# A fused token mixer, scan and expert kernel: attention's first pass of a later batch moved into the scan steps of an earlier one

## The chip, the cores and the metric

The kernel runs as one program on one core of one Trainium2 chip. The metric is device time in microseconds: the median of 3 runs is 1213.12 us (1211.83 to 1215.1). TensorE (PE in the profile), VectorE (DVE), ScalarE (ACT), GpSimd (POOL) and SyncE (SP) each run their own list of instructions in order and wait for one another by semaphores.

## The reference, cut to what matters

Four batches of 512 image tokens of width 256 go through attention with 16 heads of 16; 77 text tokens are then appended (589 rows, computed as 590), and a state-space layer with 16 states runs over them. Two expert layers and a causal attention follow; the change does not touch them except for the zeroing of their buffers in DRAM.

```
h = attention(x)                       # softmax(q k / 4) v, 16 heads, then w_out
h = concat([h, txt])
u = layernorm(h)
xp = u @ x_proj_w.T                    # 64 for the step size, 16 for B, 16 for C
delta = softplus(xp[:64] @ dt_proj_w.T + dt_proj_b)
for each t:  s = exp(delta*A)*s + delta*B_t*u_t ;  y_t = sum_n s*C_t
h = h + y + u * D_skip
h = h + one_expert(layernorm(h)) ; h = h + causal(layernorm(h)) ; h = h + two_experts(layernorm(h))
```

## The kernel before

Everything is written out by hand: each engine's list is a sequence of calls, and the semaphore waits stand in the functions. No scheduler moves anything.

**Attention of a batch** has two passes over 16 units (`NU`; 4 groups of 4 heads, `hg`, by 4 blocks of 128 tokens, `i`). In the first pass `scores` (PE, L646) writes two halves of a unit, each into a pair of PSUM banks, and `maxima` (DVE, L1588) takes the row maxima of a half. After each group `turn_maxima` (PE, L655) turns the maxima and `minus` (DVE, L1593) subtracts them inside Q. `project` (PE, L623) with `take_q` (ACT, L1163) makes Q and K of a group, `project_v` with `take_v` makes V. In the second pass `tscores` (PE, L741) makes the scores again, turned, `exps` (ACT, L1217) exponentiates them, and `weighted` (PE, L754) multiplies by V. `turn_heads`, `values`, `turn_values`, `take_vals`, `project_out` (PE, L789) and `residual` finish the batch. Then come the layer norm (`moments`, `standard_deviations`, `scales`, `normalise`), `turn_tokens`, `take_u`, `project_x`, `take_x`, `project_dt`, `softplus`, `step_size`, `input_size`.

**The scan of a batch** has 16 steps, one per state. In each, ACT makes `dA` (`decay`, L1208, L1209) and DVE runs `drive` (L1630), `recurrence` (L1639) and `output_gate` (L1649). For the first three batches POOL adds the result by DMA onto `yS` (even steps) or `yodd` (odd steps), and the gate two steps later waits for that DMA (`y_even`, `y_odd`); the last batch adds on PE. SP spreads B and C of each step over the partitions (`bc`, 4 slots).

**The order of the stages** is: first pass of batch 0 (`front(0, None)`), its second pass (`back(0, None)`), then for b = 0, 1, 2 `front(b + 1, b)`, the first pass of batch b+1 with what prepares scan b, and `back_ahead(b + 1, b)`, the second pass of batch b+1 under the 16 steps of scan b; at last scan 3 (`back(None, 3)`). The skip term u * D_skip is multiplied by PE (`skip`, L688) into the tail banks 5 to 7, and ACT copies it to `yS` (`take_y`) before POOL adds to it. `turn_both` (PE, L810, L811) turns `yS` and `yodd` back into the tail banks, and `add_y` (DVE, L1674, L1676) adds them to the hidden rows.

**The zero fills**: four DMAs (L478 to L484, the buffers of the two expert layers) are issued on SP after the load of batch 1's x.

Of the kernel before, what the change touches and what calls it, by code (L numbers as in the profile page):

```python
# [6 lines left out]
def fusion_kernel(nc, A, out):  # L7
# [41 lines left out]
    with ctx:  # L49
# [60 lines left out]
        uT = eb("uT", [P, KC, LP])  # L110
# [3 lines left out]
        eb("room", [P, 632])  # L114
# [5 lines left out]
        dBu = eb("dBu", [P, 3, KC, LP])  # L120
# [296 lines left out]
        QG = HG - 1  # L417

        def gap_bank(hg, which):
            return 5 + (2 * hg + which) % 3  # L420

        SETS = (0, 2, 5)

        def score_sets(b):
            return 3 if b == 0 else 2

        def score_banks(b, v):
            first = SETS[v % score_sets(b)]
            return slice(first, first + 2)

        def turned_banks(v):
            return slice(SETS[v % 3], SETS[v % 3] + 2)

# [12 lines left out]
        def _(q):  # L446
# [18 lines left out]
            def load_x(b):  # L465
                q.wait_ge(pe_v, 2 * b)
                q.dma_start(xT[:, :, :], A["xT"][b]).then_inc(x_in, 16)

            def spread(b, n):
                k = NS * b + n  # L470
                if k >= SLOTS:
# [6 lines left out]
            q.dma_start(xs_dram.rearrange("(j p) d -> p j d", p=P),  # L478
                        zeros[:, :].rearrange("p (o d) -> p o d", o=1).to_broadcast([P, MT, DW])).then_inc(zero_out, 16)
            q.dma_start(ys_dram.rearrange("(j p) d -> p j d", p=P),  # L480
                        zeros[:, 0:D].rearrange("p (o d) -> p o d", o=1).to_broadcast([P, G, D])).then_inc(zero_out, 16)
            q.dma_start(xs5_dram.rearrange("(j p) d -> p j d", p=P),
                        zeros[:, :].rearrange("p (o d) -> p o d", o=1).to_broadcast([P, NP2, DW])).then_inc(zero_out, 16)
            q.dma_start(ys5_dram.rearrange("(j p) d -> p j d", p=P),  # L484
                        zeros[:, 0:D].rearrange("p (o d) -> p o d", o=1).to_broadcast([P, 2 * G, D])).then_inc(zero_out, 16)
            for b in range(NB):
# [3 lines left out]
                if 0 < b < NB - 1:  # L490
                    q.wait_ge(dve_hC, NS * b)
# [110 lines left out]
        def _(pe):  # L602

            def project(b, hg, which, bank):
                if hg == 0 and which == 0:
                    pe.wait_ge(x_in, 16 * (b + 1))
                    if b == 0:
                        pe.wait_ge(wq_in, 16)
                    elif b == 1:
                        pe.wait_ge(dve_h1, 2 * b)  # L610
                    else:
                        pe.wait_ge(act_ys, b - 1)
                if b == 0 and hg == 1 and which == 0:
                    pe.wait_ge(wq_rest_in, 16)
                if b >= 2 and hg < QG and 2 * hg + which >= 3:
                    pe.wait_ge(act_q, 2 * HG * b + 2 * hg + which - 2)
                if bank == 4:
                    if which:
                        pe.wait_ge(act_q, 2 * (HG * b + hg) + 1)
                    elif hg > 1:  # L620
                        pe.wait_ge(dve_q, HG * b + hg - 1)
# [4 lines left out]
            def project_v(b, half):  # L626
                if half == 0:
                    pe.wait_ge(dve_q, HG * b + HG - 1)
                else:
                    pe.wait_ge(act_v, 2 * b + 1)  # L630
                for i in range(2):
                    for c in range(KC):
                        m = nc.tensor.matmul(ps[:, 4, D * i:D * (i + 1)], xT[:, c, P * (2 * half + i):P * (2 * half + i + 1)], wv[:, c, :],  # L633
# [1649 lines left out]
```

## Time and profile before

| | us |
|---|---|
| median of 3 runs | 1213.12 |
| span of the profiled execution | 1222.6 |
| PE, DVE, ACT busy in it | 929.1, 763.9, 440.4 |
| from the start to the end of scan 3's steps and y | 695 |
| the rest (experts, causal attention) | 527.6 |

For the profiled execution no time is given apart from its span; it is 9.5 us (0.8%) above the median of the runs. The stages before 695 us follow one another by DVE's instructions: first pass of batch 0 to 62.4, its second pass to 115, first pass of batch 1 to 181.8, scan 0 to 273.3, first pass of batch 2 to 336.2, scan 1 to 427.6, first pass of batch 3 to 490.5, scan 2 to 592.4, scan 3 to 695. A row of the view by stretches gives for each stretch the busy time of each engine, TensorE's granted clock as a share of 2.4 GHz, and the share of the DMA engines' time.

### The profile page before, as it was taken

The numbers are of one execution on the slowest core, as the hardware profiler recorded it, in microseconds if no ns is written. First come the engines' busy times: TensorE is split into PE (matmuls) and PEld (weight loads), VectorE is DVE, ScalarE is ACT, GpSimd is POOL, SyncE is SP. The second block draws the span as 40 slices with busy tenths as digits, with TensorE's granted clock in tenths as the row PEclk, the third lists the DMA queues.
The fourth block names the chain that finished last, engine by engine and source line by source line (L and its number), as shares of the span: only waits on it lengthen the run. The fifth ranks groups of instructions, "written<-read, shape, count | busy, mean of one in ns | idle before, by whom it ended". The sixth has DMA issues, their size and how long they took to land.

```text
span 1222.6 us, 14392 instructions
## 1 busy us (share of the span) xinstructions
PE 929.1 (76%) x4656; PEld 511.5 (42%) x4657; DVE 763.9 (62%) x1348; ACT 440.4 (36%) x819; POOL 205.3 (17%) x248
## 2 busy tenths in 40 slices
PE   6898989879888688974286529999588887548880
PEld 2323432334323243222253229998356565324440
DVE  4803589996899968999779931111467756732225
ACT  1174138750287501873352203444123331212220
POOL 1000001110011100111000142333000203355550
PEclk9989798976889858796687859999799998769995
DMA  3199206873058730597656436664501400249926
GB/s 100 27 326 330 84 23 160 212 166 100 18 151 206 172 109 1 135 213 159 160 181 211 148 128 192 196 195 149 233 1 46 179 6 14 75 140 398 402 75 253
DMA packets 75259, 185.57 MB, mean 152 GB/s; under 512 B 12010, under 2 KB 48573, under 8 KB 72512
## 3 DMA queue, kind: packets, MB, share of 16 engines
q1 hardware_dynamic: 60800, 148.11, 36.9%
q0 software_dynamic: 14400, 36.71, 13.7%
q8 instruction: 33, 0.54, 0.2%
q14 instruction: 26, 0.21, 0.1%
HBM read 124.88 MB, written 43.69 MB: 138 GB/s over the span
## 4 chain that ended last, share of the span: by engine, by line
PE 35%; DVE 29%; issue 19%; DMA 9%; POOL 3%; ACT 2%; another core or an unknown queue 1%; SPq 1%; POOLq 0%; DVEq 0%; ACTq 0%
DVE hst L1639 8%; PE ps L646 7%; DVE hC L1649 5%; PE ps L1139 5%; DMA bc<-bc_dram 4%; DVE mxn L1588 4%; PE ps L1015 3%; PE ps L623 3%; PE ps L1127 2%; POOL ys_dram L1546 2%; PE ps L1087 2%; DMA yodd<-hC 2%; PE ps L741 2%; DVE Hs L2170 1%; PE ps L633 1%
## 5 line engine op out<-in xcount | busy, mean ns | idle before, releaser
L1588 DVE TENSOR_REDUCE mxn<-ps 128x2 f32<-128x1024 f32 x128 | 150.6, 1220 | 60.3 <-PE ps L646 60.0
L1639 DVE TENSOR_TENSOR_SCAN hst<-dA,dBu 128x1180 f32<-128x1180 f32 x64 | 166.9, 2608 | 3.1 <-ACT dA L1209 2.6
L646 PE MATMUL ps<-Kh,Qh 32*128 32x512 f32 x512 | 122.6, 763 | 25.4 <-DVE mxn L1588 24.6
L1217 ACT ACTIVATE Ph<-ps 128x1024 f32<-128x1024 f32 x128 | 125.2, 1077 | 24.1 <-PE ps L741 23.5
L741 PE MATMUL ps<-Qh,Kh 32*128 32x512 f32 x512 | 111.0, 717 | 5.6 <-ACT Ph L1217 5.4
L1630 DVE TENSOR_TENSOR dBu<-dtu,bc 128x1180 f32<-128x1180 f32 x64 | 88.0, 1380 | 14.7 <-DMA bc<-bc_dram 14.5
L1649 DVE TENSOR_TENSOR hC<-hst,bc 128x1180 f32<-128x1180 f32 x64 | 87.2, 1362 | 9.6 <-DMA yodd<-hC 9.6
L1525 POOL DMA_DIRECT2D yS<-hC x24 | 20.8, 868 | 426.6 <-DVE hC L1649 426.6
L1139 PE MATMUL ps<-ring,xgT 128*64 128x256 f32 x512 | 70.1, 395 | 13.6 <-ACT xgT L1477 9.4
L1906 DVE TENSOR_TENSOR yo<-ps,b2r 128x256 f32<-128x256 f32 x32 | 13.6, 425 | 106.4 <-PE ps L938 106.4
L754 PE MATMUL ps<-Ph,Vh 128*32 128x512 f32 x512 | 73.7, 649 | 7.1 <-ACT OT L1221 4.4
L1208 ACT ACTIVATE dA<-delta,acol 128x590 f32<-128x590 f32 x64 | 52.2, 816 | 72.0 <-DVE hst L1639 66.1
L2163 DVE COPY yo<-ps 128x256 f32<-128x256 f32 x64 | 26.7, 423 | 77.2 <-PE ps L1139 62.3
L646 PEld LDWEIGHTS ps<-Kh,Qh 32*128 32x128 f32 x512 | 37.3, 213 | 87.2 <-DVE mxn L1588 65.7
L1577 POOL DMA_INDIRECT ys_dram<-yo,dest x64 | 62.4, 974 | 51.0 <-DVE yo L2163 31.2
L623 PE MATMUL ps<-xT,wqk 128*128 128x512 f32 x128 | 65.1, 649 | 7.6 <-DMA wqk<-in_wqk 5.6
L1557 POOL DMA_INDIRECT xs_dram<-xa,to x40 | 39.5, 988 | 175.1 <-DVE to L2005 161.9
L741 PEld LDWEIGHTS ps<-Qh,Kh 32*128 32x128 f32 x512 | 32.9, 202 | 80.8 <-ACT Ph L1217 42.0
L928 PEld LDWEIGHTS ps<-xgT,W 128*128 128x128 f32 x512 | 63.7, 196 | 3.4 <-ACT xgT L1354 1.8
L928 PE MATMUL ps<-xgT,W 128*128 128x128 f32 x512 | 64.3, 280 | 1.0 <-ACT xgT L1354 1.0
L763 PE MATMUL ps<-hC,ident 128*128 128x512 f32 (+1 forms) x96 | 45.8, 628 | 19.6 <-DVE hC L1649 19.6
L938 PE MATMUL ps<-W,hidT 128*128 x256 | 60.4, 379 | 0.0
(263 smaller groups left out, 1443.8 us busy)
## 6 DMA issues: line engine op xcount, KB each, us to landing
bc<-bc_dram SPq DMA_DIRECT2D x64, 590.0 KB, 5.9
ring<-in_we SPq DMA_DIRECT2D x16, 2048.0 KB
W<-in_w SPq DMA_DIRECT2D x46, 512.0 KB, 5.9
yS<-hC POOLq DMA_DIRECT2D x24, 590.0 KB, 7.9
yodd<-hC POOLq DMA_DIRECT2D x24, 590.0 KB, 7.8
xs_dram<-zeros SPq DMA_DIRECT2D x1, 8224.0 KB, 43.8
xg<-xs_dram SPq DMA_DIRECT2D x16, 514.0 KB
ys_dram<-zeros SPq DMA_DIRECT2D x1, 5120.0 KB, 48.3
```

The source lines that it names most:

```text
L623: m = nc.tensor.matmul(ps[:, bank, :], wqk[:, hg, which, c, :], xT[:, c, :], start=(c == 0), stop=(c == KC - 1))
L646: m = nc.tensor.matmul(ps[:, banks.start + hh % 2, :], Qh[HR * hh:HR * (hh + 1), hg, P * i:P * (i + 1)], Kh[HR * hh:HR * (hh + 1), hg, :], ...
L741: m = nc.tensor.matmul(ps[:, banks.start + hh % 2, :], Kh[HR * hh:HR * (hh + 1), hg, P * j:P * (j + 1)], Qh[HR * hh:HR * (hh + 1), hg, :], ...
L754: m = nc.tensor.matmul(ps[HR * hh:HR * (hh + 1), 4, :], Vh[:, j, 4 * hg + hh, :], Ph[:, n % 2, hh, :], start=(j == 0), stop=(j == QT - 1))
L928: m = nc.tensor.matmul(ps[:, 2 + u, P * f:P * (f + 1)], W1[:, v, c, P * f:P * (f + 1)], xgT[:, u, c, :], start=(c == 0), stop=(c == KC - 1))
L1139: t = nc.tensor.matmul(ps[CAP * k:CAP * (k + 1), 2 + j % 4, 0:D], xgT5[:, j % 2, c, CAP * k:CAP * (k + 1)], weights_of(g % PLACES)[:, 2 * ...
L1217: nc.scalar.activation(Ph[:, n % 2, 2 * g:2 * g + 2, :], ps[:, turned_banks(2 * n + g), :], ACT.Exp, scale=float(HD) ** -0.5).then_inc(act ...
L1577: nc.gpsimd.indirect_dma_start(ys5_dram, bass.IndirectOffsetOnAxis(dest5[:, j:j + 1], 0), yo5[:, j // GP % YG, j % GP, :], None, bounds_ch ...
L1588: nc.vector.tensor_reduce(slots32(mxn[:, hg % 2, i, :])[:, 2 * g:2 * g + 2, HD], ps[:, score_banks(b, 2 * (QT * hg + i) + g), :], AX.X, AL ...
L1630: nc.vector.tensor_tensor(dBu[:, k % 3, :, :], dtu[:, :, :], bc[:, k % SLOTS, 0:1, :].to_broadcast([P, KC, LP]), ALU.mult).then_inc(dve_dB ...
L1639: nc.vector.tensor_tensor_scan(hst[:, k % 2, :, :].rearrange("p c t -> p (c t)"), dA[:, k % 2, :, :].rearrange("p c t -> p (c t)"), dBu[:, ...
L1649: nc.vector.tensor_tensor(hC[:, k % 2, :, :], hst[:, k % 2, :, :], bc[:, k % SLOTS, 1:2, :].to_broadcast([P, KC, LP]), ALU.mult).then_inc( ...
```

## The change

1. The first pass of a batch no longer has a stage of its own, except batch 0's (`first_maxima`). Units 0 to 4 of batch 1 run under the second pass of batch 0, units 5 to 11 between it and scan 0 (`first_attention`), and units 12 to 15 in steps 0 to 3 of scan 0. Steps 4 to 15 of scan b take units 0 to 11 of batch b+2, steps 0 to 3 of the next scan its units 12 to 15 (`unit_at`, `LAG`).
2. From batch 1 on, all halves use one pair of banks (6, 7), except odd halves of units 6 to 11 of batch 1; projections and turned maxima use bank 5. The second pass has two pairs (0, 1 and 2, 3) where it had three.
3. In a scan step DVE runs `maxima` before `recurrence` and again before `output_gate`; `drive` of the next step moves to the end of the step. `dBu` has 2 buffers for 3, `uT` 2 for 1.
4. Skip term: `skip` and `take_y` of batches 0 to 2 go. `turn_both` multiplies u by the diagonal of D as a third matmul, in three rounds (tokens 0 to 255, 256 to 511, the text rows), in steps 1 and 2 of the next scan; `add_y` has a part for each round. POOL's first two transfers of a scan are plain copies that wait for the last round.
5. The four zero fills are issued on ACT, behind the scale of A and ahead of `take_q(0, 1, 0)`, and no longer on SP. SP no longer waits for the end of a scan before the next one's first spreads.

ScalarE at the start of the program, before (Q and K are the outputs of `take_q`, group 0, then group 1 and on):

```order
L1163 ACTIVATE Qh<-ps,bqk 128x512 [waits pe_q,pool_init,bqk_in]
L1163 ACTIVATE Kh<-ps,bqk 128x512 [waits pe_q]
L1485 ACTIVATE acol<-alog 128x32 [waits consts_in]
L1163 ACTIVATE Qh<-ps,bqk 128x512 [waits pe_q]
L1163 ACTIVATE Kh<-ps,bqk 128x512 [waits pe_q]
```

ScalarE at the same place, after:

```order
L1233 ACTIVATE Qh<-ps,bqk 128x512 [waits pe_q,pool_init,bqk_in]
L1233 ACTIVATE Kh<-ps,bqk 128x512 [waits pe_q]
L1542 ACTIVATE acol<-alog 128x32 [waits consts_in]
L1543 DMA xs_dram<-zeros 128x32x257
L1545 DMA ys_dram<-zeros 128x20x256
L1547 DMA xs_dram<-zeros 128x64x257
L1549 DMA ys_dram<-zeros 128x40x256
L1233 ACTIVATE Qh<-ps,bqk 128x512 [waits pe_q]
```

The four transfers now stand between the two groups' Q and K.

VectorE in the first steps of scan 0, before (no maxima stand between scans):

```order
L1630 TENSOR_TENSOR dBu<-dtu,bc 128x1180 [waits dve_scan,bc_in2]
L1639 SCALAR_TENSOR_TENSOR hst<-dA,dBu 128x1180 [waits dve_hC,act_dA,dve_dBu]
L1649 TENSOR_TENSOR hC<-hst,bc 128x1180 [waits y_even,dve_scan]
L1630 TENSOR_TENSOR dBu<-dtu,bc 128x1180 [waits dve_scan,bc_in3]
L1639 SCALAR_TENSOR_TENSOR hst<-dA,dBu 128x1180 [waits dve_hC,act_dA,dve_dBu]
```

VectorE in steps 1 and 2 of scan 1, after (mxn are maxima, Hs the rows that a round of y is added to):

```order
L1646 TENSOR_REDUCE mxn<-ps 128x2 [waits pe_s]
L1697 SCALAR_TENSOR_TENSOR hst<-dA,dBu 128x1180 [waits dve_hC,act_dA,dve_dBu]
L1646 TENSOR_REDUCE mxn<-ps 128x2 [waits pe_s]
L1707 TENSOR_TENSOR hC<-hst,bc 128x1180 [waits y_even,dve_scan]
L1735 TENSOR_TENSOR Hs<-Hs,ps 128x512 [waits pe_yt]
L1688 TENSOR_TENSOR dBu<-dtu,bc 128x1180 [waits dve_scan,bc_in2]
L1646 TENSOR_REDUCE mxn<-ps 128x2 [waits pe_s]
L1697 SCALAR_TENSOR_TENSOR hst<-dA,dBu 128x1180 [waits dve_hC,act_dA,dve_dBu]
L1735 TENSOR_TENSOR Hs<-Hs,ps 128x512 [waits pe_yt]
L1646 TENSOR_REDUCE mxn<-ps 128x2 [waits pe_s]
```

Two maxima and, here, a round of y have joined each step; each waits for PE.

TensorE around the second round of y in step 1 of scan 1, after (L664 are scores, L748 turned scores, L762 the weighted sum, L826 to L828 the turning of y):

```order
L664 MATMUL ps<-Kh,Qh 128x512 [waits dve_max]
L664 MATMUL ps<-Kh,Qh 128x512
L748 MATMUL ps<-Qh,Kh 128x512 [waits act_p]
L748 MATMUL ps<-Qh,Kh 128x512
L762 MATMUL ps<-Ph,Vh 32x512 [waits act_p]
L762 MATMUL ps<-Ph,Vh 32x512 x3
L826 MATMUL ps<-ident,yS 128x128 [waits dve_h2]
L827 MATMUL ps<-ident,yodd 128x128
L828 MATMUL ps<-dskd,uT 128x128
```

The round waits on DVE's previous `add_y`, and the next step's scores are queued behind it; in the old order nothing of a scan step stood behind a turning.

The diff, cut to its core:

```diff
@@ banks
-        SETS = (0, 2, 5)
+        OWN, SPARE = (6, 7), (3, 4)
+        MISC = 5
+        LAG = 4
+        SOLO = 5
+        Y_ROUNDS = ((0, 2), (2, 4), (4, 5))
+        def score_pair(b, u, g):
+            if b == 0:
+                return FIRST_SETS[(2 * u + g) % 3]
+            return SPARE if b == 1 and g == 1 and SOLO < u < NU - LAG else OWN
+        def unit_at(eb, n):
+            return (eb, NU - LAG + n) if n < LAG else (eb + 1, n - LAG)
@@ sync
-            q.dma_start(xs_dram..., zeros...)
-            q.dma_start(ys_dram..., zeros...)
-            q.dma_start(xs5_dram..., zeros...)
-            q.dma_start(ys5_dram..., zeros...)
-                if 0 < b < NB - 1:
-                    q.wait_ge(dve_hC, NS * b)
@@ tensor
+            def turn_both(b, r):
+                if r == 0:
+                    pe.wait_ge(y_even, 8 * NS * (b + 1))
+                    pe.wait_ge(y_odd, 8 * NS * (b + 1))
+                if b < NB - 2:
+                    if r == 0:
+                        pe.wait_ge(dve_q, HG * (b + 2) + QT - 1)
+                    else:
+                        pe.wait_ge(dve_h2, y_count(b, r - 1))
+                elif r == 2:
+                    pe.wait_ge(dve_h2, y_count(b, 0))
...
+                        nc.tensor.matmul(dst, yS[:, c, tokens], ident[:, :], start=True, stop=False)
+                        nc.tensor.matmul(dst, yodd[:, c, tokens], ident[:, :], start=False, stop=False)
+                        m = nc.tensor.matmul(dst, uT[:, b % 2, c, tokens], dskd[:, c, :], start=False, stop=True)
+            def during_scan(cb):
+                eb, ab = cb + 1, cb + 2
+                for n in range(NS):
+                    b, v = unit_at(eb, n)
+                    units = list(units_ahead(n))
+                    for part in range(2):
+                        if b < NB:
+                            scores(b, v, part)
+                        for u in units[part:part + 1]:
+                            tscores(eb, u)
+                            if u:
+                                weighted(eb, u - 1)
+                        if part == 0:
+                            if n == 9:
+                                weighted(eb, NU - 1)
+                            if n % QT == 0 and (n < 8 or ab < NB):
+                                turn_maxima(eb if n < 8 else ab, (2, 3, 0, 1)[n // QT])
+                            if n == 11:
+                                project_out(eb, 0)
+                                project_out(eb, 1)
+                            if n == 13:
+                                turn_tokens(eb)
+                            if n == 14:
+                                project_dt(eb)
...
+                        if n % QT == 3 and ab < NB:
+                            project(ab, n // QT, part)
@@ scalar
+            act.dma_start(xs_dram..., zeros...)
+            act.dma_start(ys_dram..., zeros...)
+            act.dma_start(xs5_dram..., zeros...)
+            act.dma_start(ys5_dram..., zeros...)
+            first_maxima()
@@ scalar, at the end of a step of during_scan
+                    if n % QT == 3 and ab < NB:
+                        take_q(ab, n // QT, 0)
+                        take_q(ab, n // QT, 1)
@@ gpsimd, add_state
-                if n == 0:
-                    pool.wait_ge(act_ys, b + 1)
+                if n < 2 and b:
+                    pool.wait_ge(pe_yt, y_count(b - 1, 2))
@@ vector
+            def during_scan(cb):
+                for n in range(NS):
+                    b, v = unit_at(eb, n)
+                    if b < NB:
+                        maxima(b, v, 0)
+                    recurrence(cb, n)
+                    if n % QT == 0 and (n < 8 or ab < NB):
+                        minus(eb if n < 8 else ab, (2, 3, 0, 1)[n // QT])
...
+                    if b < NB:
+                        maxima(b, v, 1)
+                    if n:
+                        output_gate(cb, n - 1)
...
+                    if n + 1 < NS:
+                        drive(cb, n + 1)
+                    else:
+                        step_size(eb)
+                output_gate(cb, NS - 1)
+                input_size(eb)
+                drive(eb, 0)
```

## Rows read from the trace of the kernel before

**Rows 1.** The page, chain that ended last, shares by engine.

```profile
PE 35%; DVE 29%; issue 19%; DMA 9%; POOL 3%; ACT 2%; another core or an unknown queue 1%; SPq 1%; POOLq 0%; DVEq 0%; ACTq 0%
```

**Rows 2.** Busy by stretch: length, PE, PEld, DVE, ACT, POOL, PEclk, DMA share, GB/s.

```profile
62.40:115.00 52.60, 48.37 (x302) 16.80 (x295) 5.59 (x21) 34.37 (x39) 0.00 (x0) 0.92 1.09 320
115.00:181.80 66.80, 58.67 (x225) 24.62 (x228) 42.71 (x40) 19.76 (x30) 0.00 (x0) 0.88 0.26 90
181.80:273.30 91.50, 75.76 (x354) 27.28 (x346) 87.22 (x69) 65.16 (x87) 12.84 (x15) 0.85 0.74 176
273.30:336.20 62.90, 55.47 (x216) 25.66 (x218) 46.58 (x54) 7.26 (x12) 0.86 (x1) 0.74 0.22 63
336.20:427.60 91.40, 71.65 (x354) 26.03 (x346) 87.45 (x69) 65.82 (x87) 12.57 (x15) 0.89 0.74 176
490.50:592.40 101.90, 67.19 (x322) 24.70 (x314) 90.29 (x71) 63.39 (x84) 13.43 (x16) 0.73 0.76 181
```

**Rows 3.** What DVE waited for, whole span: us in total, times, longest.

```profile
DVE mxn L1588 <- PE ps L646: 60.0, 46, 6.9
DVE rsum L1658 <- PE ps L771: 42.9, 1, 42.9
```

**Rows 4.** SP's queue in order of time: start us, us, what.

```profile
57.55 0.43 SPq L478 DMA_DIRECT2D xs_dram<-zeros  x1
58.02 10.21 SPq L480 DMA_DIRECT2D ys_dram<-zeros  x1
68.27 8.86 SPq L482 DMA_DIRECT2D xs_dram<-zeros  x1
77.17 27.73 SPq L484 DMA_DIRECT2D ys_dram<-zeros  x1
```

**Rows 5.** The page's DMA issues: KB each, us from issue to landing.

```profile
ys_dram<-zeros SPq DMA_DIRECT2D x1, 5120.0 KB, 48.3
```

**Rows 6.** ACT in order of time, at the start of the program.

```profile
13.51 0.23 ACT L1485 ACTIVATE acol<-alog 128x32 f32<-128x32 f32 x1 [1.85 <-DMA alog<-in_alog]
20.13 0.69 ACT L1163 ACTIVATE Qh<-ps,bqk 128x512 f32<-128x512 f32 x1 [6.39 <-PE ps L623]
```

**Rows 7.** DVE in order of time: maxima, a `minus`, a scan step, scan 0's first recurrence.

```profile
24.18 4.62 DVE L1588 TENSOR_REDUCE mxn<-ps 128x2 f32<-128x1024 f32 x4 [0.63 <-PE ps L646]
28.72 0.68 DVE L1593 TENSOR_TENSOR Qh<-Qh,ps 128x512 f32<-128x512 f32 x1
...
184.35 2.61 DVE L1639 TENSOR_TENSOR_SCAN hst<-dA,dBu 128x1180 f32<-128x1180 f32 x1
...
193.26 2.61 DVE L1639 TENSOR_TENSOR_SCAN hst<-dA,dBu 128x1180 f32<-128x1180 f32 x1
195.78 1.36 DVE L1649 TENSOR_TENSOR hC<-hst,bc 128x1180 f32<-128x1180 f32 x1
197.06 1.38 DVE L1630 TENSOR_TENSOR dBu<-dtu,bc 128x1180 f32<-128x1180 f32 x1
```

**Rows 8.** PE in order of time, at either clock.

```profile
21.09 1.98 PE L623 MATMUL ps<-xT,wqk 128*128 128x512 f32 x4
78.77 1.14 PE L741 MATMUL ps<-Qh,Kh 32*128 32x512 f32 x8
79.84 1.06 PE L754 MATMUL ps<-Ph,Vh 128*32 128x512 f32 x8
192.83 2.09 PE L741 MATMUL ps<-Qh,Kh 32*128 32x512 f32 x8
194.85 1.94 PE L754 MATMUL ps<-Ph,Vh 128*32 128x512 f32 x8
238.00 5.25 PE L789 MATMUL ps<-wo,valsT 128*128 128x256 f32 x16
```

**Rows 9.** What DVE waited for in scan 2, its steps (493.1 to 577) and its end.

```profile
DVE dBu L1630 <- DMA bc<-bc_dram: 4.8, 5, 1.7
...
DVE hC L1649 <- DMA yodd<-hC: 6.5, 1, 6.5
```

More of the change, by code:

```diff
@@ L602, in _, with project @@
         def _(pe):
-            def project(b, hg, which, bank):
+            def project(b, hg, which):
+                bank = MISC if b else which if hg == 0 else 4
                 if hg == 0 and which == 0:
@@ new lines, in skip, with first_maxima @@
+                        nc.tensor.matmul(tail[:, lo:hi], dskd[:, c, :], uT[:, b % 2, c, lo - c * LP:hi - c * LP],
+                                         start=(lo % S == 0 or lo == S), stop=False, skip_group_check=True)
+            def first_maxima():
+                b = 0
+                project(b, 0, 0)
+                project(b, 0, 1)
+                pe.wait_ge(consts_in, 16 * N_CONSTS)
+                for c in range(KC):
+                    m = nc.tensor.matmul(ps[:, 7, 0:D], bvb[:, c, :], wo[:, c, :], start=(c == 0), stop=(c == KC - 1))
+                m.then_inc(pe_bo, 1)
+                for u in range(NU):
+                    hg, i = u // QT, u % QT
+                    scores(b, u, 0)
+                    scores(b, u, 1)
+                    if i == 0 and hg:
+                        turn_maxima(b, hg - 1)
+                    if i in (1, 2):
+                        if hg + 1 < HG:
+                            project(b, hg + 1, i - 1)
+                        else:
+                            project_v(b, i - 1)
+                turn_maxima(b, HG - 1)
@@ new lines, in last_scan @@
+            def last_scan():
+                b = NB - 1
+                skip(b)
+                for r in range(len(Y_ROUNDS)):
+                    turn_both(b - 1, r)
+                for n in range(NS):
+                    if 0 <= n - 1 < NPF:
+                        route_turn(n - 1)
+                    if 0 <= n - 2 < NPF:
+                        route_logits(n - 2)
+                    if n == 11:
+                        route_rank(0)
+                    if n >= 2:
+                        add_state(b, n - 2)
+                add_state(b, NS - 2)
+                add_state(b, NS - 1)
+                turn_y(b)
@@ L1160, in _, with take_q @@
         def _(act):
-            def take_q(b, hg, which, bank):
+            def take_q(b, hg, which):
+                bank = MISC if b else which if hg == 0 else 4
                 act.wait_ge(pe_q, 2 * (HG * b + hg) + which + 1)
@@ L1703, in back_ahead, with first_attention @@
-            def back_ahead(eb, cb):
-                drive(cb, 0)
-                for n in range(NS):
-                    if n + 1 < NS:
-                        drive(cb, n + 1)
+                    unit_maxima(0, u)
+                    if u % QT == 0 and u:
+                        minus(0, u // QT - 1)
+                minus(0, HG - 1)
+            def first_attention():
+                for u in range(SOLO):
+                    unit_maxima(1, u)
+                minus(1, 0)
+                maxima(1, 5, 0)
+                values(0)
+                maxima(1, 5, 1)
+                maxima(1, 6, 0)
+                residual(0)
+                moments(0)
+                maxima(1, 6, 1)
+                maxima(1, 7, 0)
+                scales(0)
+                maxima(1, 7, 1)
+                maxima(1, 8, 0)
+                minus(1, 1)
+                maxima(1, 8, 1)
+                unit_maxima(1, 9)
+                unit_maxima(1, 10)
+                step_size(0)
+                maxima(1, 11, 0)
+                input_size(0)
+                maxima(1, 11, 1)
+                drive(0, 0)
```

629 lines of the change are left out of this document (295 added, 334 removed).

## The prediction

> **What bounds the kernel now.** I read the chain of waits first: PE 35% and DVE 29% of it, ACT 2% [rows 1], so the end is set by PE and DVE handing work to each other. The view by stretches then shows two kinds of stage. In a scan DVE is busy 87.2 of 91.5 us [rows 2]: it is the bound. In a first pass between scans DVE is busy 46.6 of 62.9 us, in batch 1's 42.7 of 66.8 [rows 2]; the waits say for what: 60.0 us in 46 waits of the maxima on the scores [rows 3]. Under the second pass of batch 0 DVE is busy 5.6 of 52.6 us, with one wait of 42.9 us [rows 2, 3]. So DVE idles in the first passes and in the first attention, not in the scans, and the change puts the first passes into the scans. The SP queue has its own reading: the four zero fills keep it for 10.2, 8.9 and 27.7 us each after a first of 0.4 [rows 4]. On SP nobody waited.
>
> **Zero fills on ScalarE: +41.** The four are issued one after another, each starting where the one before ends [rows 4]: 57.55 to 104.90, 47.3 us. The last one landed 48.3 us after its start [rows 5], that is at 125.5, and the DMA share in that stretch is 1.09 [rows 2]. So the issuing queue is held while the DMA engines are full; it is not a matter of an instruction's own cost. Queues run in order, so whatever stands behind these on an engine waits. In the new order that is `take_q(0, 1, 0)`. ACT would be free for the DMAs at 13.8 (scale of A from 13.51, 0.23 long) and is needed again at 20.13 [rows 6]. Held from 13.8 for 47.3 us it is free at 61.1: 41.0 us late. What is queued behind: PE's `project(0, 1, 1)` waits for that Q, and behind it all scores from the second half of group 0 on, so DVE's maxima run dry. Nothing covers it: no other work of the first pass is ready. The bounds are 0 (ACT's queue takes the DMAs as the first was taken, 0.43 each, done by 15.6, before 20.13) and 41; the nearest rows, the same four transfers in the same order, stand at 41, and I take that. That SP loses them is worth nothing: its next transfer is B and C of batch 0, after `take_x`.
>
> The Trainium skill, page "DMA: Bandwidth & Descriptors", section "Issuing engines are not separate DMA queues", says that starting DMAs on several engines saves only the sequencer's time of starting them, which is usually small relative to the DMA itself. By that rule the hold would be near 0 and the sum 41 lower. The trace disagrees for these transfers: the last held its queue 27.7 of its 48.3 us.
>
> **From the end of the first pass to scan 0: -14.** Before, scan 0's first recurrence starts at 184.35 [rows 7]. After, PE is the bound of the first attention: it is busy 48.4 of 52.6 already [rows 2]. It gets 10 halves of scores (a half is half of the 1.14 of the same shape [rows 8]: 5.7 us), 4 projections of 1.92 (the 1.98 less an overlap: 7.7) and two waits of 2 for ACT's copy: 17 us longer. Two bank pairs for three cost little: while ACT exponentiates a half (34.4 us for 39 instructions [rows 2], 0.9 each) PE fills the other in 0.57. In the stretch behind it, 66.8 long with PE busy 58.7 [rows 2], PE loses those 13.4 us, units 12 to 15 (4.6), the skip (about 2.3, the columns of 1.2 projections) and two turns of maxima (1.3): 21.6; that is the least it gets shorter. The most is 36: 18 of 32 halves go, and DVE's 24 idle us there with them as far as they were waits for scores. Net the bounds are -5 and -19. The chain of layer norm, u, x and step size keeps its order in it, and the last group's Q, K and V still go one by one through PE and ACT (four times 1.9 + 0.7); I take -14, nearer the end that takes the waits away, since the remaining halves of units 6 to 11 still alternate two bank pairs.
>
> **Scans 0 and 1: -12.7 and -3.2.** A step of DVE alone is 5.10 us: recurrence 2.52 and gate 1.28 from start to start, drive 1.30 (its 1.38 less the same overlap) [rows 7]. Two maxima at 1.15 (4.62 for 4) make it 7.4. The floor of the new stage is the DVE work of the two old ones [rows 2]. Scan 1: 87.5 + 46.6 = 134.1 against 91.4 + 62.9 = 154.3 (batch 3's first pass taken as batch 2's). Scan 0 has no y of an earlier batch to add; that work is 46.6 less 32 maxima (36.8), 4 `minus` (0.6 each, 2.4) and two operations of a drive's shape (2.8): 4.6. So its floor is 129.2 against 154.4. What is late on top of that, in one scan:
> - Steps 4 and 8 open a head group whose Q and K are copied at the end of the step before, behind that step's Exps: maxima 1.15, scores 0.57, unit of the second pass 2.07 (1.07 + 1.00 [rows 8]), two Exps 1.8, copy 0.69 [rows 6], projection 1.92, copy 0.69, scores 0.57 = 9.5 for a step of 7.4: 2.1 twice, 4.2.
> - Step 11: the second half's scores stand behind the projection out (twice a projection's columns, so 3.8 at full clock; 5.25 in the row [rows 8]) and a projection: 1.4 to 5.3 late, taken 3.
> - Steps 13 and 14, the same behind u, x and step size: 2.
> - The last gate waits for the DMA of step 13, as it did 6.5 us in scan 2 [rows 9]; the maxima now stand between, so 1.5.
> - At a scan's start the clock can be at the lower level, as in the rows at 192.83 and 194.85 [rows 8], where a step of PE (scores 2.09, 1.78 units at 3.9) is 9.0, over 7.4: 1.8 for one step.
>
> Sum 12.5. In scan 1 the three rounds of y add 4.5: round 1 waits for DVE's add at the end of step 1, a full round follows (the 12 matmuls of 128 columns and their weights, some 2.6), and the next scores stand behind it; step 2 the same. Scan 0: 129.2 + 12.5 = 141.7, -12.7; scan 1: 134.1 + 17 = 151.1, -3.2. Bounds: with no lateness -25.2 and -20.2; with PE at the lower clock through steps 0 to 8, 9 x 1.6 = 14 more each. The skip matmuls and the ACT copies that go were beside maxima and cost nothing.
>
> **Scan 2: +14.9.** No batch 4 exists, so only 8 maxima (9.2), 2 `minus` (1.2) and the y of batch 1 (4.6) join 90.3: floor 105.3 against 101.9. Lateness: y 4.5, last gate 4 (of 0 to 6.5), spreads 3 (they were 4.8 [rows 9], and the steps are short again): 11.5. So 116.8, +14.9; bounds +3.4 and +20.
>
> **Scan 3: +1.7.** The first drive now belongs to the stage before (-1.3); the y of batch 2 is turned after its last DMA has landed, with DVE's two adds at step 1, a step earlier than before: +3 (0 to 6). The rest of the kernel, 527.6 us, is unchanged: 0.
>
> **Sum.** 41.0 - 14 - 12.7 - 3.2 + 14.9 + 1.7 = +27.7. The profiled span would go from 1222.6 to 1250.3; the runs' median lies 9.5 below that execution, and the same difference gives 1213.1 + 27.7 = 1240.8, so 1241.
>
> **Rivals.**
> - *The hold does not occur on ScalarE* (chance 0.15). For it: no row shows a DMA issued there, and the first transfer took 0.43 us. Against: rows 4, the same transfers. Then 1241 - 41 = 1200; with the lateness cut too, down to 1160. The page's rule above is this rival.
> - *The hold occurs, but the steps are DVE-bound with little lateness* (0.10). For it: PE at full clock needs 1.14 + 1.78 x 2.07 = 4.8 of 7.4 us a step. All floors give -19 - 25.2 - 20.2 + 3.4 - 1.3 = -62, with the hold -21: 1192, and half the lateness 1215.
> - *TensorE falls to the lower clock in the scans* (0.12), ending slower still: scores alone between 273.3 and 336.2 had a mean of 0.74 [rows 2], and the new steps thin PE out. From 7.4 us on PE's 9.0 decides: 14 + 14 and up to 9 before scan 0 (-14 to -5): 1241 + 37 = 1278; 1260 if half of it comes.
> - *The edit of stages gives nothing at all* (0.05): the hold alone, 1254.
>
> The forecast as worked out, 1218 to 1260, has 0.58. The range that should hold the time 8 in 10 is 1193 to 1260: it takes in the first two rivals' middles and leaves out the full lower clock and the deepest gains. Within 0.3% is 1209.5 to 1216.8, what a measurement can hardly tell from no change: 0.05. Faster: 0.13 of the first rival and 0.07 of the second, 0.20. Slower: 0.75.
>
> **What would show it.** In the new profile: the four DMA issues on ACT's queue, 47 us in sum, the fourth near 28; group 1's first Q copy at about 61 and not 20; one DVE wait of about 40 us on scores near 22. DVE's first recurrence at about 184 - 14 + 41 = 211; from there to the next scan's 142, then 151, then 117. Maxima waiting on scores at steps 4, 8, 11 of scans 0 and 1 and at steps 2 and 3 behind y. Wrong if ACT's issues are under 1 us each (then 1200), or if a scan stage takes over 160 with PE at 0.5.

## The result, and the profile after

The changed kernel took 1270.47 us (median of 4, 1265.57 to 1274.11) beside 1212.47 of the kernel before: 1.048, interval 1.0446 to 1.0521, slower. I had forecast 1241. Four more executions gave 1263.1 beside 1212.65, 1.044 (1.0405 to 1.0482). So the change costs 50 to 58 us, not 28; the direction was right, and the time lies outside my range of 1193 to 1260.

The chain of waits of the changed kernel, shares of the span; ACT's queue, which had no share [rows 1], now has 4%:

```profile
PE 40%; DVE 27%; issue 17%; DMA 4%; ACTq 4%; POOL 3%; ACT 3%; another core or an unknown queue 1%; SPq 1%; POOLq 0%; DVEq 0%
```

ACT and its queue at the start of the program (start us, us, what), to be read against [rows 4, 6]:

```profile
12.12 0.23 ACT L1542 ACTIVATE acol<-alog 128x32 f32<-128x32 f32 x1 [0.81 <-DMA alog<-in_alog]
12.12 0.44 ACTq L1543 DMA_DIRECT2D xs_dram<-zeros  x1
12.60 9.28 ACTq L1545 DMA_DIRECT2D ys_dram<-zeros  x1
21.91 8.49 ACTq L1547 DMA_DIRECT2D xs_dram<-zeros  x1
30.43 28.20 ACTq L1549 DMA_DIRECT2D ys_dram<-zeros  x1
58.67 0.69 ACT L1233 ACTIVATE Qh<-ps,bqk 128x512 f32<-128x512 f32 x1 [46.33 <-issue]
```

The four issues follow one another to 58.6, and the first Q copy of group 1 stands behind them: 58.67 and not 20.13. "46.33 <-issue" is how such a hold shows: the engine sat idle and no releaser is named, and what fills the idle time are rows of its own queue. DVE ran dry behind it (DVE in order of time):

```profile
64.45 4.62 DVE L1646 TENSOR_REDUCE mxn<-ps 128x2 f32<-128x1024 f32 x4 [42.29 <-PE ps L664]
```

The stretches (columns as in [rows 2]): batch 0's first pass while held, its remainder, the first attention, the stretch to scan 0's first recurrence, scans 0, 1, 2, and 3 to its last recurrence.

```profile
13.80:62.40 48.60, 8.48 (x32) 2.78 (x24) 7.01 (x7) 0.69 (x1) 0.00 (x0) 0.59 1.09 299
62.40:102.60 40.20, 34.52 (x157) 14.04 (x160) 32.46 (x30) 4.63 (x7) 0.00 (x0) 0.97 0.46 157
102.60:161.90 59.30, 53.22 (x317) 15.96 (x309) 13.04 (x13) 34.68 (x39) 0.00 (x0) 0.98 0.00 1
161.90:215.00 53.10, 45.88 (x178) 22.30 (x174) 27.84 (x40) 17.00 (x27) 0.00 (x0) 0.84 0.16 55
215.00:361.00 146.00, 119.25 (x517) 45.79 (x514) 128.96 (x108) 75.34 (x99) 13.29 (x16) 0.83 0.52 126
361.00:521.40 160.40, 130.76 (x574) 55.74 (x574) 133.19 (x124) 72.86 (x97) 13.09 (x16) 0.81 0.50 125
521.40:644.40 123.00, 79.92 (x414) 36.66 (x414) 105.68 (x98) 64.87 (x87) 13.10 (x16) 0.79 0.64 163
644.40:732.00 87.60, 57.50 (x231) 37.13 (x231) 81.21 (x68) 30.82 (x51) 0.98 (x1) 0.81 0.59 198
```

The DVE work of scans 0 and 1, 129.0 and 133.2, is what I had summed as floors (129.2, 134.1); what is long is the rest. DVE's waits in scans 0, 1 and 2, one row each (us, times, longest):

```profile
DVE mxn L1646 <- PE ps L664: 20.0, 9, 5.3
DVE mxn L1646 <- PE ps L664: 26.9, 10, 5.3
DVE mxn L1646 <- PE ps L664: 13.1, 4, 5.3
```

(3.1 of the first stand just ahead of scan 0's first recurrence.) Two such waits. First, step 11 of scan 0 on PE in order of time: the second half's scores, at 315.15, stand behind a projection out at the lower clock and a projection, and DVE's maxima start at 316.32 after 5.29 us.

```profile
305.02 2.08 PE L664 MATMUL ps<-Kh,Qh 32*128 32x512 f32 x4
307.02 6.48 PE L795 MATMUL ps<-wo,valsT 128*128 128x256 f32 x16
313.34 1.88 PE L637 MATMUL ps<-xT,wqk 128*128 128x512 f32 x4
315.15 1.13 PE L664 MATMUL ps<-Kh,Qh 32*128 32x512 f32 x4
```

Second, step 1 of scan 1: round 0 of y holds PE from 370.92 to 375.2 ahead of scores, and rounds 1 and 2 each wait for DVE's add of the round before, while the next scores stand behind them.

```profile
376.46 1.23 DVE L1646 TENSOR_REDUCE mxn<-ps 128x2 f32<-128x1024 f32 x1 [5.25 <-PE ps L664]
...
383.68 1.23 DVE L1646 TENSOR_REDUCE mxn<-ps 128x2 f32<-128x1024 f32 x1 [2.81 <-PE ps L664]
...
392.14 1.23 DVE L1646 TENSOR_REDUCE mxn<-ps 128x2 f32<-128x1024 f32 x1 [4.14 <-PE ps L664]
```

```profile
370.92 0.80 PE L826 MATMUL ps<-ident,yS 128*128 128x128 f32 x2
...
379.63 0.49 PE L826 MATMUL ps<-ident,yS 128*128 128x128 f32 x2 [1.36 <-DVE Hs L1735]
...
388.06 0.71 PE L826 MATMUL ps<-ident,yS 128*78 128x128 f32 x2 [2.58 <-DVE Hs L1735]
```

### The profile page after: what moved, and what is told of

The parts are those of the page before. It is cut to its first block, busy times and chain, and to the rows that moved or that the text cites. A ratio compares the mean times of both kernels' runs of the same rounds, so it can differ in the third digit from the quotient of the medians.

```text
span 1265.5 us, 14467 instructions
## 1 busy us (share of the span) xinstructions
PE 927.3 (73%) x4692; PEld 517.8 (41%) x4693; DVE 763.7 (60%) x1351; ACT 440.6 (35%) x816; POOL 204.0 (16%) x248
## 4 chain that ended last, share of the span: by engine, by line
PE 40%; DVE 27%; issue 17%; DMA 4%; ACTq 4%; POOL 3%; ACT 3%; another core or an unknown queue 1%; SPq 1%; POOLq 0%; DVEq 0%
DVE hst L1697 7%; PE ps L664 6%; PE ps L1209 5%; DVE mxn L1646 4%; PE ps L637 4%; DVE hC L1707 3%; PE ps L748 3%; PE ps L1085 3%; PE ps L762 3%; ACTq L1549 2%; PE ps L1197 2%; PE ps L1157 2%; POOL ys_dram L1604 2%; DVE dBu L1688 2%; DMA yodd<-hC 1%
## 5 line engine op out<-in xcount | busy, mean ns | idle before, releaser
L1646 DVE TENSOR_REDUCE mxn<-ps 128x2 f32<-128x1024 f32 x128 | 154.1, 1219 | 173.0 <-PE ps L664 172.9
L664 PE MATMUL ps<-Kh,Qh 32*128 32x512 f32 x512 | 149.0, 723 | 53.9 <-DVE mxn L1646 46.0
L748 PE MATMUL ps<-Qh,Kh 32*128 32x512 f32 x512 | 132.7, 700 | 4.9 <-ACT Ph L1289 4.7
L637 PE MATMUL ps<-xT,wqk 128*128 128x512 f32 x128 | 71.1, 685 | 53.0 <-ACT Qh L1233 46.8
L664 PEld LDWEIGHTS ps<-Kh,Qh 32*128 32x128 f32 x512 | 40.0, 206 | 130.7 <-DVE mxn L1646 88.2
L762 PE MATMUL ps<-Ph,Vh 128*32 128x512 f32 x512 | 75.1, 662 | 1.3 <-ACT Ph L1289 1.3
L1635 POOL DMA_INDIRECT ys_dram<-yo,dest x64 | 62.2, 972 | 47.1 <-DVE yo L2266 26.7
L748 PEld LDWEIGHTS ps<-Qh,Kh 32*128 32x128 f32 x512 | 44.5, 207 | 46.7 <-issue 23.3
L637 PEld LDWEIGHTS ps<-xT,wqk 128*128 128x128 f32 x128 | 24.7, 212 | 94.4 <-ACT Qh L1233 57.6
```

The costliest lines, as they stand in the source:

```text
L637: m = nc.tensor.matmul(ps[:, bank, :], wqk[:, hg, which, c, :], xT[:, c, :], start=(c == 0), stop=(c == KC - 1))
L664: m = nc.tensor.matmul(ps[:, banks.start + hh % 2, :], Qh[HR * hh:HR * (hh + 1), hg, P * i:P * (i + 1)], Kh[HR * hh:HR * (hh + 1), hg, :], ...
L748: m = nc.tensor.matmul(ps[:, banks.start + hh % 2, :], Kh[HR * hh:HR * (hh + 1), hg, P * j:P * (j + 1)], Qh[HR * hh:HR * (hh + 1), hg, :], ...
L762: m = nc.tensor.matmul(ps[HR * hh:HR * (hh + 1), 4, :], Vh[:, j, 4 * hg + hh, :], Ph[:, n % 2, hh, :], start=(j == 0), stop=(j == QT - 1))
L1635: nc.gpsimd.indirect_dma_start(ys5_dram, bass.IndirectOffsetOnAxis(dest5[:, j:j + 1], 0), yo5[:, j // GP % YG, j % GP, :], None, bounds_ch ...
L1646: nc.vector.tensor_reduce(slots32(mxn[:, hg % 2, i, :])[:, 2 * g:2 * g + 2, HD], ps[:, score_banks(b, u, g), :], AX.X, ALU.max, negate=Tru ...
```

## The experiments

**e1, e2: the fills alone.** e1 is the changed kernel with them on SP, e2 the kernel before with them on ScalarE.

```diff
-            act.dma_start(xs_dram..., zeros...)      # e1: these four go
+            q.dma_start(xs_dram..., zeros...)        # e1: behind load_x(1), on SP; e2 the reverse
```

> The changed kernel with its four zero fills issued from SP's queue again, behind the load of batch 1, all else as changed. Theory A (the issues hold ScalarE's queue, and all behind it is late by that): the first pass of batch 0 ends 40.2 us earlier, at 62.4, nothing behind it gives that back, and the time is 1270.5 - 40.2 = 1230. Theory B (the fills cost by their traffic, wherever they are issued): the first pass keeps most of the 40 us and the time stays near 1270. Either way what is over 1212.5 is the price of the rest of the change: 18 us by A.

> The kernel before with one part of the change alone: the four zero fills issued by ScalarE behind the scale of A, ahead of the Q copies. Theory A: ScalarE held from 12.1 to 58.6 as in the changed kernel, 40 us on the end of the first pass, 1212.5 + 40 = 1252.5. Theory B: the hold costs only together with the new stages (the old ones would take it in their idle time): under 10 us, near 1215.

e1: 1222.8, 1.009 of before (1.0054 to 1.0124). Its first pass ends at 61.9, as before, and all stages behind are those of the changed kernel within 3.1 us. e2: 1247.9, 1.030 (1.0234 to 1.0356), its first pass ends 36.4 later. ScalarE's queue in e2:

```profile
12.47 8.84 ACTq L1480 DMA_DIRECT2D ys_dram<-zeros  x1
21.34 8.05 ACTq L1482 DMA_DIRECT2D xs_dram<-zeros  x1
29.42 25.31 ACTq L1484 DMA_DIRECT2D ys_dram<-zeros  x1
54.77 0.69 ACT L1155 ACTIVATE Qh<-ps,bqk 128x512 f32<-128x512 f32 x1 [42.56 <-issue]
```

Theory A stands both ways. Over the kernel before, the hold costs 37 us in the old order (e2, +36.9) and 39 to 46 in the new (+50.5 or +58.0, less e1's +11.8); the end of the first pass moves by 36 and 40. The traffic by itself cost nothing that is seen. The rest of the change costs 12 us, where I had forecast a gain of 13.

**e5: the changed kernel again.** No edit.

> The changed kernel, unchanged, beside the others of this call, to have its time and the kernel's before over more executions on one chip. If the 15 us between the difference of the two profiled executions (+42.9) and of the medians (+58.0) is scatter between executions, more of them give between the two, near 1211 + 50; if it is steady, +58 again.

1263.1, +50.5: the first reading. Scan 1 took 154.9 here, at a granted clock of 0.85, and 160.4 at 0.81 in the first profile, of the same kernel.

**e6: two fills on ScalarE, two on SP.**

```diff
-            act.dma_start(xs5_dram...)  act.dma_start(ys5_dram...)
+            q.dma_start(xs5_dram...)    q.dma_start(ys5_dram...)
```

> The changed kernel with the first two zero fills on ScalarE as in it and the last two on SP. Theory A (each issue is held until the transfer before it has been worked off, so the second takes 9.3, the third and fourth 8.5 and 28.2): ScalarE free at 22 where it is needed at 20.1, 1.8 late, some 1224. Theory B (the hold depends on all the bytes under way, from whichever queue): SP's two make the second issue on ScalarE longer, up to the 37 us of the four: 1224 to 1260.

1230.9, 1.016 (1.0126 to 1.0187). ScalarE and its queue:

```profile
13.15 0.44 ACTq L1547 DMA_DIRECT2D xs_dram<-zeros  x1
13.63 8.80 ACTq L1549 DMA_DIRECT2D ys_dram<-zeros  x1
22.48 0.69 ACT L1237 ACTIVATE Qh<-ps,bqk 128x512 f32<-128x512 f32 x1 [9.10 <-issue]
```

The second issue is held nearly as long as with all four on the queue (8.80 for 9.28), and the first pass ends at 65.2, 3.3 late. Theory B was not put to the test: SP issued its two from 61.33 us on, 39 us after ScalarE was free, so none of SP's fills was under way beside them. They show the same once more: the first of them (8.2 MB) took SP's queue 0.43, the second 25.4. The first issue on a queue is nearly free, the next ones are held. The time is 7 over theory A's 1224; the first pass, 3.3 late for 1.8, explains 1.5 of that, the rest stays open.

**e3: one bank pair in the kernel before**, for the scores of batches 2 and 3.

```diff
-            return 3 if b == 0 else 2
+            return 3 if b == 0 else 2 if b == 1 else 1
```

> The kernel before with the scores of batches 2 and 3 on one pair of banks instead of two in turn, so that the two halves of a unit are issued apart, each behind the maxima of the other. Theory A (a half that is issued by itself takes TensorE 1.1 us, as long as both halves issued together): a half costs 1.15 of maxima, 1.13 of scores and some 0.1 between them, 32 halves 76 us against a first pass of 62.9: 13 longer in each of two, 1238. Theory B (a half is half of the 1.14, 0.57): 32 x 1.8 = 58, under the 62.9 that the stage takes for other reasons: 0 to +3, 1212 to 1216.

1326.1, 1.092: stages 0 and 1 took 212.4 and 211.7 for 154, 58 longer each. Both theories missed the size; A's direction holds. PE in order of time:

```profile
305.87 2.08 PE L646 MATMUL ps<-Kh,Qh 32*128 32x512 f32 x4 [1.33 <-DVE mxn L1588]
...
309.27 2.08 PE L646 MATMUL ps<-Kh,Qh 32*128 32x512 f32 x4 [1.33 <-DVE mxn L1588]
```

A half by itself (x4) takes 2.08, what both halves (x8) of the same shape take at that clock in [rows 8]; a half goes round in 3.40, not the 2.4 I expected: the granted clock was 0.50 from 300 to 320 us, and PE stood idle 1.33 of each 3.40 of these rows. I had priced the alternation at the higher clock; at the lower 32 x 3.40 = 109 for 62.9, and more where y and projections stand between.

**e4: the y rounds' matmuls** cut to 3 a round on top of e1 (the kernel leaves out most of y of batches 0 and 1).

```diff
-                for i in range(first, last):
+                for i in range(first, last if b == NB - 2 else first + 1):
```

> As the first of these (fills on SP), and the matmuls that add and turn y of batches 0 and 1 cut from 12, 12 and 6 to 3 in each round (so most of that y is left out); the waits of the rounds, the adds of DVE and the order stay. Theory A (the three rounds' matmuls on TensorE, at either clock, stand ahead of scores for 12 us a scan in scans 1 and 2): some 10 less in each, 20 under the first kernel, 1210. Theory B (they cost the 4.5 that I put in the sum): 4 less in each, 1222. Theory C (it is the wait of a round for DVE's add, not the matmuls): hardly any change, 1228.

1214.6, 8 under e1; scan 2 went from 123.2 to 116.8, scan 1 from 160.4 to 154.9. Since e5 has 154.9 in scan 1 with all matmuls in, only scan 2's 6.4 (four executions of three kernels with the full rounds gave 123.0 to 123.2) is shown. That is between A and B. The maxima of scan 2 waited 8.4 in place of 13.1, and the last gate's wait of 2 for a DMA was gone; the 8.4 stay with the order.

**e7, e8: the late steps and the rounds' order.** e7 moves projections away from steps 7 and 11 and the Q copy ahead of the second unit's Exps; e8 also moves rounds 1 and 2 by half a step.

```diff
-                        if n % QT == 3 and ab < NB:
+                        if n in (3, 6, 10, 15) and ab < NB:          # V: both halves in step 9
...
-                            for r in ((0, 1), (2, None))[n - 1][part:part + 1]:
+                            for r in ((0, None), (1, 2))[n - 1][part:part + 1]:   # e8
```

> Fills on SP, and in the scans the first pass's projections placed away from the late steps: Q and K of the second head group at step 6 for 7, V in one step (9), Q and K of the third at step 10 for 11, where the projection out stands, and the Q copies at steps 3 and 6 between the two units' Exps. Theory A (steps 4, 8 and 11 are late, 2.8, 2.7 and 5.3 us, by what stands ahead of their scores on TensorE and ScalarE): about 6 to 7 of these 10.8 go in each of scans 0 and 1, 13 in all, 1222.8 - 13 = 1210. Theory B (TensorE is the bound over these steps, so the wait turns up at another): 0 to -3, 1220 to 1223.

> As e7, and the second and third rounds of y half a step later: the second ahead of the second unit part of step 2, the third behind it, so that neither waits for DVE's add of the round before while scores stand behind it. Theory A (the wait of a round for the add is a part of the y rounds' 10 to 12 us): 2 to 3 less in each of scans 1 and 2, 5 under e7. Theory B (TensorE's work alone decides, at the lower clock at a scan's start): no difference from e7.

e7: 1212.2, 0.999 (0.9969 to 1.002), 10.6 under e1; scan 0 fell from 146.0 to 141.1, scan 1 to 150.3. In scan 0 the wait of step 4 went from 2.8 to 1.8, those of steps 8 and 11 (2.7 and 5.3) are gone, and two of about 1 at step 6 came. Mostly A. e8: 1197.3, 0.990 (0.9843 to 0.9956). Its scan 2 took 114.2 for 120.2: the same matmuls, and 6 us less. What DVE's maxima waited for in e7 and then e8, 460 to 580 us (scan 2 starts at 468.5 and 460.6; 1.3 of the first row stand at the end of scan 1):

```profile
DVE mxn L1652 <- PE ps L672: 11.9, 5, 4.3
```

```profile
DVE mxn L1652 <- PE ps L672: 5.2, 2, 4.3
```

So in scan 2 the handing over between PE's rounds and DVE's adds cost as much as the matmuls; A, and larger than I had expected of it. In scan 1 no gain is shown. The waits of steps 1 and 2 went there too (2.8 and 2.7), but in two of three executions of this kernel (e8, e9, e14) that of step 6 grew from 0.7 to 3.4, and scan 1 took 148.7, 150.3 and 150.3 for e7's 150.3; since e7's had a granted clock of 0.85 and theirs 0.82, whether the order gives nothing there or the clock took it back stays open. Nor are the 15 us between the medians of e7 and e8 the edit's: scan 0, which it does not touch, took 136.1 in e8's profile and 141.1 in those of e7, e9 and e14.

**e9 to e12.** e9 is e8 again; e10 and e11 keep PE busy with dropped matmuls in its waits; e12 moves round 0 too.

```diff
+                        if part and n in (0,):          # e11: (0, 12)
+                            keep_busy(4 if n == 0 else 6)
...
-                            for r in ((0, None), (1, 2))[n - 1][part:part + 1]:
+                            for r in ((None, 0), (1, 2))[n - 1][part:part + 1]:   # e12
```

> e8 unchanged, over five rounds, since its one profiled execution was also shorter in stages that its edit does not touch (scan 0 by 5.0, the stretch ahead of it by 3.9 against e7). Theory A: the edit gives 6 in scan 2 and some 4 in scan 1, 10 under e7, 1202. Theory B (e8's 1197 is what it is): 1197. Both below the kernel before at 1211 to 1213.

> e8 with four matmuls of 128 x 512 into an unused bank, their result dropped, in TensorE's wait of 4.1 us ahead of the second score half of step 0 of scans 0, 1 and 2. Theory A (TensorE goes on at the lower clock because it stood idle there, and the scores, the turned scores and the first y round of step 1 then take 2.08, 3.8 and 4.2 us for 1.13, 2.0 and 2.6): the granted clock of the ten us behind rises from 0.5, and 3 to 5 us go in each of the three scans, 1197 - 12 = 1185. Theory B (the clock there has been lowered by what was before and does not come back by this): no gain, 1197, or a loss of 1 each where the four run at the lower clock and outlast the wait: 1200.

> As e10, with six more such matmuls in the wait of 5.6 us ahead of the second score half of step 12 in scans 0 and 1. Theory A: turning the tokens, the x projection (4.34 us in the row, for some 2.3) and the step size projection run at the higher clock, the waits of step 13 (1.0 to 1.5) go, 1 to 2 under e10 in each of two scans: 1182. Theory B: no difference from e10, or 1 to 2 more.

> As e8, with the first round of y half a step later too, behind the second score half of step 1. Theory A (the 4.3 to 5.2 us wait of step 1 is the round standing ahead of scores): that wait falls to about 1, of which the scores of step 2, now right behind the round, give back some 2: 2 less in each of scans 1 and 2, 1193. Theory B (TensorE is the bound from step 0 to step 3 whatever the order): 1197.

These ran on a chip where the kernel before took 1192.2, so only ratios are compared (the stages up to scan 3 took what they do elsewhere; the difference is in the rest, 513 in e9 and 536 in e14): e9 0.988 (0.9846 to 0.9913), e10 0.991, e11 0.991, e12 0.989, the last three within e9's interval. e8 stays under the kernel before. PE in e10, at the start of scan 1:

```profile
304.70 3.60 PE L885 MATMUL ps<-wqk 128*128 128x512 f32 x8
308.96 1.13 PE L672 MATMUL ps<-Kh,Qh 32*128 32x512 f32 x4 [0.66 <-DVE mxn L1658]
313.19 1.22 PE L672 MATMUL ps<-Kh,Qh 32*128 32x512 f32 x2 [3.11 <-DVE mxn L1658]
```

With the filler in the wait the next half ran at the higher clock, 1.13 (in e8, behind a wait of 4.09, it took 2.07), but behind the next wait, 3.11, the units ran at the lower clock as in e8: theory B in the time. In e12 step 1's wait on scores fell from 4.3 to 1.5, and DVE waited 2.2 for the round in its add: the wait changed its place, B again.

**e13, e14: three pairs.** What was still open was the stretch ahead of scan 0. e14 is e8 beside it.

```diff
+                scores(1, 6, 1)
                 project_out(0, 0)
                 project_out(0, 1)
-                scores(1, 6, 1)
...
+                scores(1, 8, 1)
                 turn_maxima(1, 1)
-                scores(1, 8, 1)        # and (11, 1) ahead of project(1, 3, 1)
```

> As e8, with the two halves of batch 1's units 6, 8 and 11, which have a bank pair each, issued back to back in the stretch behind the first attention, and the projections out, the turned maxima and the K projection that stood between them behind both. Nothing is added or removed. Theory A (a half issued alone takes TensorE as long as both together, 1.13 at the higher clock and 2.08 at the lower, not half of it, and that is what the prediction missed in this stretch): three such halves go, 1.13 + 2.08 + 1.13 = 4.3 of TensorE, of which 2 to 4 on the path, since it is busy 48.7 of 57.0 there; the stretch from the end of the first pass to the first recurrence falls from 112 or 116 to about 110 or 113. Theory B (a half costs the same wherever it stands): no change, or 1 to 2 longer where DVE now waits for the projection out.

> e8 unchanged, on the same chip as e13, since e13's edit is worth a few us and the same kernel took 112 in one profiled execution and 116 in another over the stretch in question: about 0.988 of the kernel before, as it was.

e13 0.988 (0.9839 to 0.9918), e14 0.9935 (0.9902 to 0.9967): the intervals overlap, and the medians are 1199.5 and 1200.85, so the times alone show no difference. (e14, forecast at 0.988, came out nearer to 1.) From the first pass's end to the first recurrence the two took 111.4 and 114.7, closer than e8 and e9, which are one kernel (112.2 and 116.1). The traces are clearer where they are cut at the end of the first attention. From there to the first recurrence (columns as in [rows 2]), e14 and then e13:

```profile
122.10:174.92 52.82, 45.62 (x174) 22.34 (x174) 27.70 (x39) 16.97 (x27) 0.00 (x0) 0.84 0.15 55
```

```profile
124.80:173.13 48.33, 40.69 (x176) 21.18 (x174) 27.61 (x39) 16.97 (x27) 0.00 (x0) 0.89 0.16 59
```

This part took 52.8 to 53.3 in each of the twelve profiled executions of the changed order without e13's edit, and 48.3 with it: 4.5 less, with TensorE busy 4.9 less. The scatter stands in the first attention itself, 58.3 to 63.6. PE in e14 and in e13, unit 8:

```profile
145.95 2.08 PE L672 MATMUL ps<-Kh,Qh 32*128 32x512 f32 x4
147.96 1.11 PE L690 MATMUL ps<-ident,mxn 128*128 128x128 f32 x4
149.00 2.08 PE L672 MATMUL ps<-Kh,Qh 32*128 32x512 f32 x4
```

```profile
148.69 2.09 PE L672 MATMUL ps<-Kh,Qh 32*128 32x512 f32 x8
150.72 1.11 PE L690 MATMUL ps<-ident,mxn 128*128 128x128 f32 x4
```

Two halves apart: 4.16. Back to back: 2.09. Theory A, in the trace. Three halves are 4.3 of the 4.9; the rest goes with the higher granted clock, 0.89 for 0.84. e8 and all that is built on it stay under the kernel before, by 0.7 to 1.2%.

## Why the prediction was wrong, step by step

The direction was right by the hold alone: without it I had forecast a gain of 13 and measured a loss of 12 (e1). Single profiled executions of one kernel differ by up to 6 us in one stage, so I take means: of the old order over the kernel before, e2 and e3 (in stages that their edits leave alone), of the new over the first profile, e1, e5 and e6. Stages run between first recurrences.

| stage | old, us | new, us | difference | predicted |
|---|---|---|---|---|
| first pass to its last `minus` | 61.9 | 101.9 | +40.0 | +41 |
| to scan 0 | 119.9 | 115.1 | -4.8 | -14 |
| scan 0 | 154.1 | 145.6 | -8.5 | -12.7 |
| scan 1 | 155.2 | 158.1 | +2.9 | -3.2 |
| scan 2 | 99.7 | 123.1 | +23.4 | +14.9 |
| scan 3, to its last recurrence | 89.7 | 87.7 | -2.0 | +1.7 |
| rest | 533.4 | 534.0 | +0.6 | 0 |
| sum | | | +51.6 | +27.7 |

Of the 23.9 missed, 14.6 stand in scans 1 and 2, 9.2 in the stretch to scan 0 and 4.2 in scan 0; the hold, scan 3 and the rest give 4.1 back.

- **The hold (+41) was right**, in mechanism and size (+40.0), against the rival without it: e1 and e2. Here the Trainium skill, page "DMA: Bandwidth & Descriptors", section "Issuing engines are not separate DMA queues", has the starting of a DMA cost a usually small sequencer time; the rows bear that out for the first issue (0.44) and not for those behind it (9.3, 8.5, 28.2).
- **In the stretch to scan 0 the step that failed is "a half is half of the 1.14"**, and with it the choice of -14. A half issued alone takes 1.13 or 2.08, as long as the pair. The Trainium skill, page "TensorEngine Tiling (Array Packing)", section "Key Properties", says that tiles of the array can run matmuls in parallel; the rows agree (x8 in 1.14, x4 in 1.13), and read ahead of the prediction it would have spoken against halving. So would the trace of the kernel before: from 115 to 181.8 its scores took TensorE 26.7 us for 32 halves, 0.83 each.

  To compare my two parts, the stage has to be cut at the same work, the last weighted sum of batch 0: the 52.6 of [rows 2] also hold the turning of the heads and the projection out, which now stand behind the first attention. Cut there, in means over the same executions, the first attention grew from 40.0 to 61.4, by 21.5 where I had 17, and the stretch behind it fell from 79.3 to 53.0, by 26.3 where I had 31. In the first part a half straight ahead of turned scores runs partly within them: a unit with one takes 2.9 to 3.2 for 2.07, so 0.8 to 1.1 for a half and not 0.57, by this estimate some 4 over the ten, about what was missed. In the second part, in the first profile, 8 halves between 161.9 and 215 stand alone, five at 1.13 and three at 2.08: 11.9 where eight at 0.57 are 4.6. e13 shows that this lies on the path, by undoing three for 4.5 us.

  That is not a full account of the second part. The halves that left it had cost more than 0.57 too, so the scores fell by 10.0 (26.7 to 16.7) for the 10.3 of the sum: there two errors met, which is luck. All of TensorE's work fell by 24.4 (70.2 to 45.8) for 21.6, and what did not come is the going of its waits: 10.7 to 7.2 in the first two profiles, where -31 needed 9.4 less.
- **The y rounds were mis-sized, and this is the larger step that failed**: 4.5 where maxima waited 12.2 (5.25 + 2.81 + 4.14) in scan 1, and the same within 0.1 in scan 2. The sum has rounds 1 and 2, at the higher clock, and nothing for round 0, which held TensorE for 4.3 ahead of scores at a clock that starts low; and there are two waits for an add (1.36, 2.58). In scan 2 this is 7.7 of the 8.5 missed, and e4 and e8 take 6 us of it away each. The other terms of scan 2 nearly cancel, which is luck: the last gate waited 2.1 for the 4 that I had put, the spreads nothing for 3, against a wait of 1.5 for the softplus and the base's 2.2. In scan 1, 6.1 were missed, and part of its 5.25 is the slow start of a scan, for which the sum has 1.8. There the size is read from the waits alone: scan 1 took 154.9 in e4 as in e5 with the full rounds, and 150.3 in e7 as in e9 and e14 with the other order.
- **Scan 0's lateness**: 16.9 for 12.5. Steps 4 and 8 had 2.77 and 2.73 (2.1 each), step 11 5.29 (3: I had taken the middle of 1.4 to 5.3), the start 1.72 and 1.43 (1.8), step 13 1.51 (2 for steps 13 and 14); the last gate waited for nothing (1.5). Steps 4 and 8 each have two halves in their chain, so the price of a half fails here too. The floors were right to 1 us.
- **Scan 3** gained where I put +3: its y waits came (2.6 and 2.0), but old waits of its start, for dA and for bc, went.
- **The lower clock** came only for some units at a time (0.79 to 0.83 over scans 0 to 2), not through whole scans: the rival at 1278 did not happen, though the time is near it, and scan 1's 160.4 had a clock of 0.81, not the 0.5 of my sign. e3 is what it looks like.
- **The base**: the first profiled execution of the kernel before was 9.5 over its median; the old order's means put 2.6, 2.2 and 4.8 of that in the stretch to scan 0, in scan 2 and in the rest. So gains read against that one execution were too large by this much. The runs' +50.5 lies near the table's +51.6; what the +58.0 of the first runs holds beyond that stays open as scatter between executions.

## What to carry to other kernels

A DMA issue is a place in its engine's program: put large ones where nothing behind them on that engine is needed, or issue one and no second. Before pricing part of an operation as its fraction, find a row of that part issued alone: two head halves in different row groups of TensorE cost together what one costs by itself. Where two engines hand one bank to and fro in rounds, count every hand-over, and put other work between a round and the add it waits for: in scan 2 that order was worth as much as the matmuls. Cut stages at the same work before and after, or a piece that changed its stage hides what was gained.

## What the runs showed of the hardware

- ScalarE's queue took the first fill (4.1 MB) in 0.44 us and held the engine 9.3, 8.5 and 28.2 us for the next three (2.6, 8.2 and 5.1 MB), as SP's had (10.2, 8.9, 27.7). Split two and two over the queues (e6), the first of each took 0.44 and 0.43, the second 8.8 and 25.4.
- Four matmuls of 32 rows in four row groups (x8 in the rows, each is recorded twice) took 1.14 us (2.09 at the lower clock), two of them alone (x4) 1.13 (2.08).
- With TensorE kept busy for 3.6 us, the next half ran at the higher clock (1.13) where it had run at the lower (2.07) behind a wait of 4.1; behind the following wait (3.1, and 2.2 without that work) the clock was low in both.
- The same kernel's profiled executions took 58.3 or 62.5 us in the first attention at granted clocks of 1.00 and 0.93, and 136.1 or 141.1 in scan 0 at 0.87 and 0.82 (e8, e9), and the stretch between them 53.3 and 52.9. Differences under 5 us in a stage need a second execution, or a cut at a piece that does not scatter.
